# Attention inside a language-model layer: query and key projections as three float32r terms, and another order of the ring items

## The reference

```python
q = jnp.einsum('bsd,hde->bshe', x, W_Q) + b_Q
k = jnp.einsum('bsd,hde->bshe', x, W_K) + b_K
v = jnp.einsum('bsd,hde->bshe', x, W_V) + b_V
scores = jnp.einsum('bqhe,bkhe->bhqk', q, k) / math.sqrt(D_HEAD)
scores = jnp.where(causal[None, None], scores, -jnp.inf)
pattern = jax.nn.softmax(scores, axis=-1)
z = jnp.einsum('bhqk,bkhe->bqhe', pattern, v)
attn_out = jnp.einsum('bqhe,hed->bqd', z, W_O) + b_O
```

## Time and profile before

| | us |
|---|---|
| median of three runs | 2647.95 |
| the profiled execution | 2648.46 |
| its span, first to last instruction | 2646.7 |
| PE busy | 2390.5 (90%) |
| DVE busy | 1859.5 (70%) |
| ACT busy | 1231.6 (47%) |
| POOL busy | 1242.6 (47%) |
| one unit of attention (from the first side item of step 6 to that of the next unit) | 126.93 |

### The profile page before, as it was taken

How to read it: one execution, slowest core, us unless ns; L and a number is a source line. 1 busy time by engine, 2 the same in 40 slices (tenths; PEclk the granted TensorE clock), 3 DMA queues, 4 the chain that set the end, 5 groups by cost and what they waited for, 6 DMA issues and landing times. The chain is left out here.

```text
span 2646.7 us, 42215 instructions
## 1 busy us (share of the span) xinstructions
PE 2390.5 (90%) x16000; PEld 1225.3 (46%) x16000; DVE 1859.5 (70%) x3771; ACT 1231.6 (47%) x1728; POOL 1242.6 (47%) x858
## 2 busy tenths in 40 slices
PE   3565899999999999999999999996999999999998
PEld 1233555555555555555555556543333333333332
DVE  7864565656565656566565656687988989888987
ACT  3422233333333333333333333354777777777776
POOL 5000265756575757575756666663413323324120
PEclk9787899999999999999999999996999999999999
DMA  1002000000001000000000001131011000000000
GB/s 50 12 23 61 1 8 8 3 9 1 10 1 33 1 10 1 10 1 10 1 9 1 3 1 20 19 53 55 9 19 21 15 19 21 15 19 9 19 7 7
DMA packets 42940, 39.33 MB, mean 15 GB/s; under 512 B 26865, under 2 KB 35186, under 8 KB 41842
## 3 DMA queue, kind: packets, MB, share of 16 engines
q1 hardware_dynamic: 40608, 31.18, 5.3%
q0 software_dynamic: 1536, 3.15, 0.4%
q10 hardware_dynamic: 594, 2.31, 0.2%
HBM read 26.13 MB, written 10.49 MB: 14 GB/s over the span
## 5 line engine op out<-in xcount | busy, mean ns | idle before, releaser
L678 POOL TENSOR_TENSOR acc<-acc,pT 128x1024 f32<-128x1024 f32 (+3 forms) x412 | 836.0, 2029 | 239.7 <-ACT pT L1077 202.9
L1077 ACT ACTIVATE pT<-banks 128x1024 f32<-128x1024 f32 x480 | 406.7, 896 | 812.9 <-PE banks L751 747.2
L1806 DVE TENSOR_TENSOR hw<-hid,banks 128x512 f32<-128x512 f32 x1024 | 662.8, 680 | 84.0 <-PE banks L1489 69.6
L896 DVE TENSOR_REDUCE part<-banks 128x2 f32<-128x1024 f32 (+3 forms) x432 | 438.0, 1044 | 313.0 <-PE banks L727 311.3
L1648 ACT ACTIVATE hid<-banks 128x1024 f32<-128x1024 f32 x512 | 496.7, 1022 | 183.8 <-PE banks L1479 167.4
L767 PE MATMUL banks<-pT,v 128*64 128x512 f32 (+3 forms) x1920 | 405.5, 543 | 1.1 <-POOL pT L662 1.1
L1489 PE MATMUL banks<-wT,select 64*128 64x512 f16 x1024 | 341.6, 392 | 42.1 <-DVE hw L1806 22.5
L1479 PE MATMUL banks<-zst,w1c 50*128 50x512 f32 x1024 | 306.5, 541 | 10.7 <-ACT hid L1648 10.7
L1497 PE MATMUL banks<-hw,w 128*32 128x512 f32 x2048 | 278.3, 616 | 0.8 <-DVE hw L1806 0.8
L1489 PEld LDWEIGHTS banks<-wT,select 64*128 64x128 f16 x1024 | 93.7, 94 | 399.1 <-DVE hw L1806 340.2
L767 PEld LDWEIGHTS banks<-pT,v 128*64 128x64 f32 x1920 | 116.7, 136 | 203.1 <-issue 181.1
(11 more groups left out here) (228 smaller groups left out, 3161.4 us busy)
## 6 DMA issues: line engine op xcount, KB each, us to landing
zst<-z_scratch SPq DMA_DIRECT2D x48, 128.0 KB, 4.0
z_scratch<-zp SPq DMA_DIRECT2D x8, 512.0 KB, 2.8
out_h<-o SPq DMA_DIRECT2D x8, 384.0 KB, 2.6
xT_scratch<-xs_hi SPq DMA_DIRECT2D x4, 512.0 KB, 2.7
xt_hi<-xT_scratch SPq DMA_DIRECT2D x2, 1024.0 KB, 5.7
w<-in_L_ffn_W ACTq DMA_DIRECT2D x1, 2048.0 KB, 8.5
xt_hi<-in_L_ffn_W SPq DMA_DIRECT2D x12, 128.0 KB, 4.6
v<-in_L_ffn_W SPq DMA_DIRECT2D x12, 128.0 KB, 4.3
```

The source lines that it names most:

```text
L678: pool.tensor_tensor(acc[:, G % 2, :, off:CH], acc[:, G % 2, :, off:CH], pT[:, slot, :, 0:w], ALU.add).then_inc(summed, 1)
L896: last = dve.tensor_reduce(to[:, :, c:c + 1], both[:, :, 0:whole], AX.X, ALU.max)
L1077: act.activation(pT[:, J % PSLOTS, :, 0:CH - off], both[:, :, 0:CH - off], ACT.Exp, scale=E ** -0.5)\
L1806: dve.tensor_tensor(hw[:, n % 2, q, :], hid[:, n % 2, q, :], ring_bank(("w", g, n, q)), ALU.mult).then_inc(mixed, 1)
```

## The change

**Projections of q and k.** x and the q and k weights are split into a float32r high part and a float32r remainder: ACT copies the high part, DVE subtracts it from the original. An item then consists of three float32r terms over the 128 rows and three over the 64 rows. v stays float32. The weights of q and k, high and low, are held once (not twice), so `load_weights(n + 1)` now follows the projections of unit n, and the raw weights have one buffer.

```diff
-                    for h in range(2):
-                        t = (2 * h + c) * CH
-                        pe.matmul(banks[h][:, :], w_hi[:, u, w, :], xt_hi[:, t:t + CH], start=True, stop=False)
-                    for h in range(2):
-                        part_rows = slice(h * DLO, (h + 1) * DLO)
-                        last = pe.matmul(banks[h][:, :], w_lo[part_rows, u, w, :], xt_lo[part_rows, c * CH:(c + 1) * CH],
-                                         start=False, stop=True)
+                    for k, (a, b) in enumerate(((wh_hi, xh_hi), (wl_hi, xh_hi), (wh_hi, xl_hi))):
+                        for h in range(2):
+                            t = (2 * h + c) * CH
+                            pe.matmul(banks[h][:, :], a[:, w, :], b[:, t:t + CH], start=(k == 0), stop=False)
+                    for k, (a, b) in enumerate(((wh_lo, xh_lo), (wl_lo, xh_lo), (wh_lo, xl_lo))):
+                        for h in range(2):
+                            part_rows = slice(h * DLO, (h + 1) * DLO)
+                            last = pe.matmul(banks[h][:, :], a[part_rows, w, :], b[part_rows, c * CH:(c + 1) * CH],
+                                             start=False, stop=(k == 2))
```

```diff
+            def split_x_low(b, k):
...
+                dve.wait_ge(x_high, 4 * b + k + 1)
...
+                dve.tensor_tensor(low, raw, high.bitcast(F32), ALU.subtract).then_inc(x_low, 1)
+
+            def split_w_low(n):
+                dve.wait_ge(w_high, 2 * n + 2)
+                for raw, high, low in ((w_hi, wh_hi, wl_hi), (w_lo, wh_lo, wl_lo)):
+                    dve.tensor_tensor(low[:, :, :], raw[:, 0:2, :], high[:, :, :].bitcast(F32), ALU.subtract)\
+                       .then_inc(w_low, 1)
...
+            split_w_low(0)
+            for k in range(4):
+                split_x_low(0, k)
             rows_of_low()
```

**The order in the ring.** The first side item of a step moves between the two s2 blocks, on PE, on ACT and in `order`:

```diff
-                order += [("s2", it, 2 * t), ("s2", it, 2 * t + 1)] + PLAN[it][t]
+                order += [("s2", it, 2 * t)] + PLAN[it][t][:1] + [("s2", it, 2 * t + 1)] + PLAN[it][t][1:]
```

More of the change, by code:

```diff
@@ L830, in _ @@
                     score_columns(it, 2 * t)
+                    for item in PLAN[it][t][:1]:
+                        side(item)
                     score_columns(it, 2 * t + 1)
-                    for item in PLAN[it][t]:
+                    for item in PLAN[it][t][1:]:
                         side(item)
@@ L867, in banks_of @@
                 return pair_of_banks[a // 2]
+            def split_x_low(b, k):
+                c, rest = divmod(k, 2)
+                dve.wait_ge(x_high, 4 * b + k + 1)
+                if rest:
+                    cols = slice(c * CH, (c + 1) * CH)
+                    raw, high, low = xt_lo[:, cols], xh_lo[:, cols], xl_lo[:, cols]
+                else:
+                    raw, high, low = (half_view(a[:, :], c) for a in (xt_hi, xh_hi, xl_hi))
+                dve.tensor_tensor(low, raw, high.bitcast(F32), ALU.subtract).then_inc(x_low, 1)
[4 more added lines that the diff above has]
+                       .then_inc(w_low, 1)
             def take_low(kind, n, c):
@@ L943, in normalise @@
                 dve.wait_ge(pv_done, it * NK + LASTKEY[Q] + 1)
-                if G >= 2:
-                    dve.wait_ge(filled, place[("out", (G - 2) // NQC, (G - 2) % NQC)] + 1)
-                dve.tensor_tensor(oT[:, G % 2, :], psum[6 + G % 2], total[:, G % 2, :], ALU.mult)\
+                dve.tensor_tensor(total[:, G % 2, :], psum[6 + G % 2], total[:, G % 2, :], ALU.mult)\
                    .then_inc(normalised, 1)
@@ L1034, in _ @@
                         side(item)
+                    if t == SPLIT_W_AT and it + 2 <= LAST:
+                        split_w_low(it + 2)
+                    if it == SPLIT_X_IN and t in SPLIT_X_AT:
+                        split_x_low(1, SPLIT_X_AT[t])
                     if it == LAST:
@@ L1057, in item_in, with split_x_high, split_w_high @@
                 return pair_of_banks[m % RING]
+            def split_x_high(b, k):
+                c, rest = divmod(k, 2)
+                act.wait_ge(x_in, 48 * b + 48)
+                if rest:
+                    cols = slice(c * CH, (c + 1) * CH)
+                    act.activation(xh_lo[:, cols], xt_lo[:, cols], ACT.Copy).then_inc(x_high, 1)
+                else:
+                    act.activation(half_view(xh_hi[:, :], c), half_view(xt_hi[:, :], c), ACT.Copy).then_inc(x_high, 1)
+            def split_w_high(n):
+                act.wait_ge(w_in, (n + 1) * 12 * 16)
+                for raw, high in ((w_hi, wh_hi), (w_lo, wh_lo)):
+                    act.activation(high[:, :, :], raw[:, 0:2, :], ACT.Copy).then_inc(w_high, 1)
             def take_high(kind, n, c):
@@ L1083, in copy_total @@
                 if G >= 2:
-                    act.wait_ge(normalised, G - 1)
+                    act.wait_ge(filled, place[("out", (G - 2) // NQC, (G - 2) % NQC)] + 1)
                 act.activation(total[:, G % 2, :], both[:, 0, :], ACT.Copy).then_inc(total_copied, 1)
@@ L1114, in side @@
                     take_high(*item)
+            split_w_high(0)
+            for k in range(4):
+                split_x_high(0, k)
             for item in first_pass(0):
                 side(item)
+            split_w_high(1)
             for it in range(UNITS):
@@ L1120, in _ @@
                     exponentials(it, 2 * t)
+                    for item in PLAN[it][t][:1]:
+                        side(item)
                     exponentials(it, 2 * t + 1)
-                    for item in PLAN[it][t]:
+                    for item in PLAN[it][t][1:]:
                         side(item)
+                    if t == SPLIT_W_AT and it + 2 <= LAST:
+                        split_w_high(it + 2)
+                    if it == SPLIT_X_IN and t in SPLIT_X_AT:
+                        split_x_high(1, SPLIT_X_AT[t])
                     if behind(it, t, 1):
```

65 lines of the change are left out of this document (38 added, 27 removed).

## The result

| | before | after |
|---|---|---|
| median, us | 2648.99 | 2686.63 (four runs, 2685.72 to 2690.12) |
| the profiled execution | 2648.46 | 2690.12 |
| its span | 2646.7 | 2688.4 |

The ratio of the times is 1.0147, 95% interval 1.0129 to 1.0164: slower by 37.6 us between the medians, 41.7 between the profiled spans. The forecast said slower by 13.4, with a range up to 2682. The direction was right, the size was not.

What follows compares the result with a forecast made beforehand. PE's work and waits bound the kernel. Projections -30.8, moved item +39.6, start +1.0, unit 0 +1.0, x of batch 1 +0.6, last unit +2.0 sum to +13.4 us: 2662 us, range 2624 to 2682.

Steps and rivals of the forecast that it cites:

- What bounds the kernel: Attention units: PE, busy 124.54 of 126.93 us; its work and waits count in full, other engines' work only where PE waits.
- An item is 2.27: 0.70 less: Steps 1 and 2: a q or k item falls from 2.97 to 2.27 us; 44 items give 30.8 us.
- 0.10 for each of two changes between the tilings: Within a q or k item: two switches between 128-row and 64-row matmuls, 0.10 us each, on top of 2.07.
- The rival of slow 128-row streams: Projections: 128-row streams miss 0.23 us through weight loads or rate; 2699 with loads exposed, more at 0.48; chance 0.07.
- The moved item, +39.6: All steps: an s1 item between the two s2 blocks brings new PE waits, 3.6 us a unit, 39.6 in 11.
- the maxima of step 14's first item: Steps 13 to 15: DVE starts them 9.34 us after step 13's start, held by POOL; +1.4 by step 15's end.
- the weights' subtraction in step 9 costs nothing: Step 9: DVE's splitting of the weights falls into its idle time; without that cover some 0.7 us a unit.
- No term for the clock: All units: the sum held nothing for a granted clock falling to half behind new waits; forecast 0.
- the wait of step 9: Step 9: s1 items wait 1.7 to 1.9 us for DVE's maxima, `out` no longer waits; step +0.4 us.
- Last unit, "+1.0 for each: +2.0": Last unit: two s2 blocks waiting for DVE to take an earlier `out` cost +1.0 each; between 0 and 5.8 together.
- Start, unit 0 and x of batch 1: Edges: start +1.0, step 0 of unit 0 +1.0, splitting x in step 13 of unit 4 +0.6 us.

Runs made afterwards that it cites:

- The run with the 64 rows first: Fastest kernel so far (2605.29 us), with a q item's 64-row matmuls ahead of its 128-row ones, the k item unchanged: 2597.66 us.
- the inverses later: Inverses, normalisation and output of column blocks 1 and 2 one macro step later: on the changed kernel 2650.87 us, with the order of before 2621.4 us.
- shortening both long waits: Changed kernel with the matmuls of one s1 item in step 9 and one in step 14 issued twice from unit 1 on: 2679.24 us.
- shortening one: Changed kernel with the six matmuls of one s1 item ahead of the long wait in step 9 issued twice: 2686.18 us.
- the run of the order alone: Kernel before, float32 projections kept, with each step's first planned item moved between its two s2 blocks: 2705.87 us, ratio 1.0211.
- the run with the old order in the last unit: Changed kernel, with both s2 blocks of a step again ahead of the other items in the last unit only: 2685.35 us.

## Why the prediction was wrong in size

- **What bounds the kernel: right.** PE's waits and PE's work in a unit, and the clock that it worked at, decided every kernel here. The order cost 57 us alone, though no engine got more work by it.
- **"An item is 2.27: 0.70 less": wrong by 0.23, 9 us in all** (by the steps an item is 0.49 less, and 44 items make 9.2 us). The rate of 0.23 a stream held (0.235 measured, over 128 rows too), and no weight load showed. What failed is "0.10 for each of two changes between the tilings". A change costs 0.1 us in the pair of streams ahead of it and another 0.1 in the pair behind it, so 0.2, and there are two an item. The run with the 64 rows first took two changes out of each pair of items, and 0.34 and 0.39 us went with them. The rival of slow 128-row streams is out. The rule of the Trainium skill on which it leaned (TensorE: Matmul & The Clock Gate, "What overlaps and what doesn't"), that a load overlaps running matmuls only with another row group, does not hold here: each of the six streams over 128 rows loads weights for all rows, and they follow each other at 0.235.
- **The moved item, +39.6: right,** as a sum (+39.4) and step by step. Each wait came where the ring's three places and DVE's durations put it. (One reading of the earlier trace rows was off, without consequence: DVE idles 40% of a unit, not a third.) That the maxima of step 14's first item are held by POOL's addition through the CAST was the dearest term, and its start came within 0.04 us. The lock of which the Trainium skill speaks (SBUF — State Buffer, "SBUF: two separate sides") agrees again: issued 0.4 us earlier, the CAST ended with POOL's addition at 780.65 to 780.67. That the weights' subtraction in step 9 costs nothing, for DVE has nothing else to do there, held in the changed kernel (0.43 us each). It fails with the inverses later, where one of the two subtractions takes 1.9 to 2.6 in units 0 to 9, ending 0.28 us behind an addition of POOL each time, and `out` waits 1.4 for what stands behind it.
- **No term for the clock: wrong by 12.8 us in the profiled execution.** The forecast had the wait of step 9 as 1.7 to 1.9 us, and it came out as 1.88, with 1.45 the longest wait in step 9 before. Behind it the granted clock fell to half in seven of ten units, and `out` and `weigh` took 2.81 and 2.33 in place of 1.57 and 1.94. A wait was priced as its own length alone. In the profiled executions, shortening both long waits took the half clocks away; shortening one moved them to the other. The trace of before had a warning that no row took up: in step 0 of unit 0 PE waits 1.91, and the float32 matmuls behind it run at half clock, 3.78 in place of the 1.98 of the earlier trace rows:

```profile
299.38 0.98 PE L735 MATMUL banks<-ident,cpad 128*128 128x128 f32 x4 [1.91 <-DVE cpad L915]
...
302.19 3.78 PE L711 MATMUL banks<-xt_hi,w_hi 128*128 128x512 f32 x4
```

- **Last unit, "+1.0 for each: +2.0": wrong by 5.** The range given for the term, 0 to 5.8, was nearer. DVE takes `out` when its own queue comes to it (1817.88 to 1818.83, without idling before; 4.48 us into step 18, before 4.93), so an earlier `out` is hardly taken earlier, and the block that waits for it stands one place further forward: the wait grew from 2.16 to 4.30. Step 3 grew by 2.34 in another way: `out` waits there for DVE's `normalise`, which comes no sooner than its inverse, and the block that used to fill this time follows it. The clock is in this term too: 1.35 of the 2.34 are `out` at half clock, and in the run of the order alone, where the clock stayed whole there, step 3 grew by 1.1 only. The sum had not counted at all the transpositions and the product in steps 9 to 11, which were moved as well (+1.1 in steps 9 to 12).
- **Start, unit 0 and x of batch 1: near as a sum,** +1.9 for a forecast of +2.6, and partly by luck. The second pass begins 2.2 us later (forecast 1.0), and step 0 of unit 0 is 1.5 longer (forecast 1.0). Step 1 of unit 0 gave 2.5 back beyond the items, which was not in the sum: most of it is the half clock of before, just shown, against a shorter one now.

Together 9.2 + 12.8 + 5.0 + 2.0 (behind the last unit) - 0.9 (start and the moved item) is 28.1 of the 28.3 by which 41.7 exceeds 13.4. All three misses were on one side, and the range, which ended at 2682, held no term for the clock at all.

That the item between the blocks is bad in itself would be a wrong reading. In steps 6, 8 and 17 it gains 0.65 us a unit, since DVE is done there. It loses where DVE is not done: behind an inverse in steps 9 and 14, which the later inverses took away, and in steps 11 and 19, which stayed as long with the inverses moved (5.38 and 5.30). There the third item comes too soon behind the first for DVE's maxima. The late inverses took 35.8 us off the new order, but the old order with the same inverses is 29.5 us faster still.

## What to carry to other kernels

Where a ring of buffers couples engines, work out for each place whose reader three places back now has to be done, and when, from the queue of that reader: it gave every wait of the units with side items to a quarter of a microsecond. Do not price a new wait by its length alone: look in the trace of before for waits of that length anywhere, and at the clock behind them. And read the cost of a change of tiling from both of its sides before multiplying it by the number of items.

## What the runs showed of the hardware

- In the units with side items, a wait of PE of 1.8 to 1.9 us in otherwise dense work was followed by half of the granted clock (the level of 1.2 GHz) in some executions of the same instructions and not in others: in step 9 of the changed kernel in seven of ten units, and then not behind the equal wait of step 14 of the same units (in unit 4 it came there too, behind 2.43); with the first wait cut to 1.2, behind the one in step 14 in seven of ten. It cost 1.5 to 1.7 us each time. Behind the waits of 1.1 to 1.7 us in steps 9 to 14 of all kernels here the clock stayed whole in every unit.
- The length of the wait alone does not decide it. In the first pass of unit 0, where PE has other, shorter waits nearby, the clock fell to half behind waits of 1.40 and 1.51 in the kernel before. It stayed whole behind 2.43 in step 14 of unit 4 in the run with the old order in the last unit, and behind 3.03 in step 3 of the last unit in the run of the order alone. Why it comes in one place and not in the next was not settled.
- A subtraction of DVE over 128x256, with both inputs in SBUF, takes 0.41 to 0.43 us by itself. In all twenty units that split weights in the two kernels with the inverses one step later, one of the two took 1.9 to 2.6 us and ended 0.28 us behind an addition of POOL.
- A change of PE between tiles of 64 and of 128 rows costs about 0.2 us in float32r: 0.1 shows in the pair of streams ahead of it (0.56 against 0.47) and 0.1 in the pair behind it (0.34 against 0.23), and two changes fewer gave back 0.34 to 0.39.
- Float32r streams of 512 columns over 128 rows follow each other every 0.235 us, each with its own weights for all 128 rows.
- The first item at the start of the attention, behind a wait of 21.85 us and at half of the granted clock, takes 4.40 us (231.58 to 235.98); the third, at the full clock, takes 2.50.
